# A second graph network whose two layers run interleaved, layer 0 of the next block ahead of layer 1 of this one

## What is computed

```python
def layer(h, params):                      # twice, weights of layer 0 and then of layer 1
    u = jnp.einsum('bid,bjd->bij', h, h) / temper
    a = jax.nn.softmax(u, axis=-1)
    delta = a * adjacency_matrix
    attn = delta / (jnp.sum(delta, axis=-1, keepdims=True) + 1e-10)
    hl, hs, hr = h @ wl.T + b_l, h @ ws.T + b_s, h @ wr.T + b_r
    ctx = (attn * upper) @ hl + diag(attn)[..., None] * hs + (attn * lower) @ hr
    o = (ctx - mean) / jnp.sqrt(var + LN_EPS) * g + beta
    return jax.nn.relu(o)
x = layernorm(x + second_network(x, adj))
```

## Time and profile before

| | |
|---|---|
| median of 3 runs | 1693.14 us (1692.88 to 1693.48) |
| the profiled execution | 1695.46 us, of which its span is 1693.6 us |
| PE busy | 1668.7 us, 99% of the span |
| DVE, ACT, POOL busy | 1267.6 us (75%), 956.0 us (56%), 623.2 us (37%) |
| chain that ended last | PE 93%, DVE 3%, ACT 1%, POOL 1%, DMA 1%, issue 1% |
| granted TensorE clock, mean | 0.995 of full speed |

### The profile page before, as it was taken

The page is one execution under the profiler, slowest core; times in us unless marked ns, Lnnn a source line. Parts: engine busy times, 40 slices in busy tenths (PEclk is TensorE's granted clock), DMA queues, the critical chain, the costliest instruction groups (busy, mean ns, idle before and its releaser), DMA issues.

```text
span 1693.6 us, 29852 instructions
## 1 busy us (share of the span) xinstructions
PE 1668.7 (99%) x9684; PEld 1580.2 (93%) x9684; DVE 1267.6 (75%) x2778; ACT 956.0 (56%) x2009; POOL 623.2 (37%) x668
## 2 busy tenths in 40 slices
PE   9999999999999999999999999999999999999995
PEld 8989989889899899899999999999999999999995
DVE  5587685867859678695887968769687686877866
ACT  5645455364554645546566665565655656656654
POOL 5243252433424233243523514434153351523505
PEclk9999999999999999999999999999999999999998
DMA  5215021020300203003104140400304004040101
GB/s 160 77 30 158 6 71 53 25 93 6 109 14 25 93 6 118 6 25 94 49 15 97 41 96 0 118 0 22 96 22 96 0 25 92 22 96 0 49 30 38
DMA packets 108074, 92.02 MB, mean 54 GB/s; under 512 B 63360, under 2 KB 101248, under 8 KB 108032
## 3 DMA queue, kind: packets, MB, share of 16 engines
q1 hardware_dynamic: 108032, 91.51, 19.1%
HBM read 66.33 MB, written 25.17 MB: 54 GB/s over the span
## 4 chain that ended last, share of the span: by engine, by line
PE 93%; DVE 3%; ACT 1%; POOL 1%; DMA 1%; issue 1%; SPq 0%; ACTq 0%; DVEq 0%
PE b_work L1228 33%; PE b_work L377 23%; PE b_work L402 11%; PE b_score_ps L392 8%; PE b_work L1241 8%; PE b_work L413 4%; PE b_score_ps L119 3%; PE b_turn L360 1%; PE b_turn L1185 1%; PE b_score_ps L1204 1%; DMA b_z<-in_L_gnn_W_lin 1%; PE b_score_ps L1201 0%; POOL g_qv_lo L663 0%; PE b_turn L1212 0%; PE b_score_ps L1185 0%
## 5 line engine op out<-in xcount | busy, mean ns | idle before, releaser
L1228 PE MATMUL b_work<-b_w_hi,b_ht 128*128 128x384 f32 x2304 | 605.2, 337 | 0.5 <-ACT b_work L1327 0.3
L1228 PEld LDWEIGHTS b_work<-b_w_hi,b_ht 128*128 128x128 f32 x2304 | 417.5, 188 | 1.7 <-ACT b_work L1327 1.2
L1228 PE MATMUL b_work<-b_w_lo,b_ht 128*128 128x384 f32 x1152 | 385.3, 334 | 0.0
L377 PE MATMUL b_work<-b_ht,b_w_hi 128*128 128x512 f32 x1134 | 350.5, 390 | 0.7 <-DVE g_qv_lo L782 0.7
L663 POOL TENSOR_TENSOR g_qv_lo<-g_v_full,g_qv_hi 128x384 fp32r<-128x384 f32 x128 | 132.8, 1057 | 359.2 <-ACT g_qv_hi L533 359.2
L377 PEld LDWEIGHTS b_work<-b_ht,b_w_hi 128*128 128x128 f32 x1134 | 211.8, 188 | 41.8 <-issue 1.1
L377 PE MATMUL b_work<-b_ht,b_w_lo 128*128 128x512 f32 x567 | 221.6, 391 | 0.0
L1228 PEld LDWEIGHTS b_work<-b_w_lo,b_ht 128*128 128x128 f32 x1152 | 216.5, 188 | 0.0
L1633 DVE TENSOR_TENSOR s_v_lo<-b_work,s_v_hi 128x384 fp32r<-128x384 f32 x256 | 140.7, 555 | 90.3 <-ACT s_v_hi L1333 86.6
L402 PE MATMUL b_work<-b_w_hi,b_ht 128*128 128x384 f32 x768 | 206.1, 335 | 0.0
L1327 ACT ACTIVATE b_work<-b_bias 128x384 f32<-128x384 f32 x256 | 126.4, 494 | 140.0 <-DVE b_z L1671 104.5
(11 more groups left out here) (174 smaller groups left out, 3288.1 us busy)
## 6 DMA issues: line engine op xcount, KB each, us to landing
g_x_res<-in_x SPq DMA_DIRECT2D x16, 768.0 KB, 7.7
b_x_in<-x SPq DMA_DIRECT2D x64, 192.0 KB, 6.7
s_x_res<-x SPq DMA_DIRECT2D x16, 768.0 KB, 7.3
b_x_in<-in_x_t SPq DMA_DIRECT2D x15, 768.0 KB, 8.9
out<-b_z SPq DMA_DIRECT2D x15, 768.0 KB, 3.8
x<-b_z SPq DMA_DIRECT2D x14, 768.0 KB, 3.9
b_a_tr<-in_adj_t SPq DMA_DIRECT2D x64, 64.0 KB, 3.3
g_a_nat<-in_adj SPq DMA_DIRECT2D x32, 64.0 KB, 2.4
```

What stands on the lines that cost most here:

```text
L377: mm = pe.matmul(bank[:], w, h, start=(n == 0), stop=(n == len(pairs) - 1))
L1228: mm = pe.matmul(bank[:, 0:H], h, w, start=(n == 0 and side == 2), stop=(n == len(pairs) - 1), skip_group_check=True)
```

## The change

- The units are ordered anew. `layer_of`, `block_of`, `stream_of` and `pair_of` now say what a unit is: serial number 0 is layer 0 of block 0; then odd units are layer 0 of block k + 1 and even units are layer 1 of block k; the last unit (number 31) is layer 1 of block 15.
- The rows between the layers of one block go from `z[1]` to a DRAM tensor `z_rows` and from there, in four DMAs, into `x_in[0]` (`pass_rows_on`), and `flip_block` turns them there, for 14 of the 16 layer-1 units. The layer-1 units 2 and 31 are still turned by TensorE (`turned_by_tensor`), from rows that `normalise` writes to `x_in`.
- In the unit ahead of a layer-1 unit the turning stands earlier on ScalarE and VectorE (`early`).
- A buffer `z[unit % 2]` holds a unit's output. `contexts_out` waits for `z_stored` in layer 0 and for the store of the previous output block in layer 1. SyncE's order, `masks` and `final_normalise` follow the new order of units.
- With the block transposes the features of layer 1 come in another order, so the layer-1 weights, gain and shift are loaded in quarters: four DMAs in place of one each.
- TensorE's pass 0 stands ahead of its loop.

```diff
             def next_tables():
+                for out_, row in ((sh.gain_f, next_ln_w[0]), (sh.shift_f, next_ln_b[0])):
+                    parts = row.rearrange("(q k p) -> q p k", q=QUADS, k=KO)
+                    for q in range(QUADS):
+                        sp.dma_start(out_[quarter(q)], parts[q], allow_slow_non_contiguous=True).then_inc(next_small, 16)
...
+    FINAL = PASSES * UNITS - 1
+
+    def serial(i, unit):
+
+        return i * UNITS + unit if isinstance(i, int) else None
+
+    def layer_of(i, unit):
+        if serial(i, unit) in (0, FINAL):
+            return int(serial(i, unit) == FINAL)
+        return 1 - unit % 2
+
+    def block_of(i, unit):
+        if serial(i, unit) in (0, FINAL):
+            return 0 if serial(i, unit) == 0 else PASSES * STREAMS - 1
+        return (i + unit // UNITS) * STREAMS + (-1, 1, 0, 2)[unit % UNITS]
+
+    def stream_of(i, unit):
+        if serial(i, unit) in (0, FINAL):
+            return int(serial(i, unit) == FINAL)
+        return (1, 1, 0, 0)[unit % UNITS]
+
+    def pair_of(i, unit):
+
+        if serial(i, unit) in (0, FINAL):
+            return (0, 0) if serial(i, unit) == 0 else (PASSES - 1, 1)
+        back, s = ((-1, 1), (0, 1), (0, 0), (1, 0))[unit % UNITS]
+        step = unit // UNITS + back
+        return (i + step if step > 0 else i - 1 if step < 0 else i), s
+
+    def turned_by_tensor(i, unit):
+
+        return serial(i, unit) in (2, FINAL)
...
+            def load_x(i, unit):
+
+                sp.wait_ge(turned, nth(i, unit - 2, KO, KO - 1))
+                for q in range(QUADS):
+                    sp.dma_start(sh.x_blocks[unit % 2][quarter(q)], x_b[(*pair_of(i, unit), q)])\
+                        .then_inc(x_loaded[unit % 2], 16)
+
+            def pass_rows_on(i, unit):
+
+                k = block_of(i, unit)
+                sp.wait_ge(z_ready, (k + 1) * NT)
+                sp.dma_start(z_v, z[unit % 2][:, :, 0:H]).then_inc(z_stored, 16)
+                sp.wait_ge(z_stored, k * 16)
+                for q in range(QUADS):
+                    sp.dma_start(sh.x_blocks[1 - unit % 2][quarter(q)], z_b[q]).then_inc(x_loaded[1 - unit % 2], 16)
 
             def load_adj(i, s):
+
+                sp.wait_ge(keep_ready[s], i + 1)
                 for b in range(2):
                     h = slice(b * 64, b * 64 + 64)
-                    sp.dma_start(a_tr[s][h, :, h], adj_t_v[i, s, b]).then_inc(adj_loaded[s], 16)
+                    sp.dma_start(a_tr[s][h, :, h], adj_t_v[i + 1, s, b]).then_inc(adj_loaded[s], 16)
+
...
+            def first_pass():
+                load_residual(0, 0)
+                load_adj(0, 0)
+                load_residual(0, 1)
+                pass_rows_on(0, 1)
+                load_x(0, 5)
+                load_adj(0, 1)
+                store_last(0)
+                store_last(1)
+
+            def one_pass(i):
+                store_out(i - 1, 2)
+                pass_rows_on(i - 1, 3)
+                load_x(i, 3)
+                load_adj(i, 0)
+                load_residual(i, 0)
+                store_out(i, 0)
+                pass_rows_on(i, 1)
+                load_x(i, 5)
+                load_adj(i, 1)
+                load_residual(i, 1)
+
...
             def turn_block(i, unit, k):
+                pe.wait_ge(z_ready, (block_of(i, unit) + 1) * NT)
                 if k < 2:
                     pe.wait_ge(prob_lo_ready, nth(i, unit - 1, 2, k))
                 else:
                     pe.wait_ge(sums_ready, nth(i, unit - 1, 1, 0))
+                rows = x_in[block_of(i, unit) % 2]
                 for t in range(NT):
-                    mm = pe.transpose(turn_banks[k][:, t * P:(t + 1) * P], z[s][:, t, k * P:(k + 1) * P], eye)
+                    mm = pe.transpose(turn_banks[k][:, t * P:(t + 1) * P], rows[:, t, k * P:(k + 1) * P], eye)
                 mm.then_inc(turned, 1)
...
             def turn_out(i, unit, k):
-                bank = turn_banks[k]
+                bank = turn_banks[k] if turned_by_tensor(i, unit) else flipped[k % 2]
...
             def normalise(i, unit, tiles):
+                    rows, out_ = z[s][:, t, 0:H], z[s][:, t, 0:H]
+                    if serial(i, unit) in (0, FINAL - 2):
+
+                        rows = rows.rearrange("p (q k f) -> p k q f", q=QUADS, k=KO)
+                        out_ = x_in[block_of(i, unit) % 2][:, t, :].rearrange("p (k q f) -> p k q f", q=QUADS, k=KO)
+                    nc.scalar.activation(out_, rows, ACT.Identity, scale=rstd[:, t:t + 1],
...
             def second_half(i, unit, more, tail):
-                flip_next = more and layer_of(unit + 1) == 0
-                turn_next = more and layer_of(unit + 1) == 1
+                turn_next = more and turned_by_tensor(i, unit + 1)
+                early = more and not turn_next and layer_of(i, unit + 1) == 1
+                late = more and layer_of(i, unit + 1) == 0
                 probabilities_hi(i, unit)
+                if early:
+                    turn_out(i, unit + 1, 0)
                 value_hi(i, unit, 6)
                 seed(i, unit, 9)
-                if flip_next:
+                if early:
+                    turn_out(i, unit + 1, 1)
+                if late:
                     turn_out(i, unit + 1, 0)
                 value_hi(i, unit, 7)
                 seed(i, unit, 10)
-                if flip_next:
+                if early:
+                    turn_out(i, unit + 1, 2)
+                if late:
                     turn_out(i, unit + 1, 1)
                 if turn_next:
                     turn_out(i, unit + 1, 0)
                     turn_out(i, unit + 1, 1)
                 value_hi(i, unit, 9)
-                if more:
+                if late or turn_next:
                     turn_out(i, unit + 1, 2)
                 value_hi(i, unit, 10)
...
             def masks(i, s, first=False):
-                    pool.wait_ge(own_ready, nth(i, 2 + s - UNITS, 1, 0))
+                    pool.wait_ge(own_ready, nth(i, 2 * s - 2, 1, 0))
...
             def one_pass(i, last, first=False):
-                    if unit == 0 and not first:
-                        final_normalise(1)
-                    if unit == UNITS - 1 and not last:
-                        final_normalise(0)
+                    if layer == 0 and not (first and unit < 3):
+                        final_normalise(unit - 1, stream_of(i, unit - 1))
...
-                    if not last and unit % STREAMS == 1:
-                        masks(i + 1, unit // STREAMS)
+                    if layer == 0 and unit > 0 and not last:
+                        masks(i + 1, unit // 2)
...
             def flip_block(i, unit, k):
+                dve.wait_ge(x_loaded[s], 16 * QUADS * (block_of(i, unit) + layer_of(i, unit)))
...
+            def contexts_out(i, unit, tiles=range(NT)):
+
+                s, k = unit % 2, block_of(i, unit)
+                if layer_of(i, unit) == 0:
+                    wait(dve, z_stored, (k - 1) * 16)
+                elif serial(i, unit) not in (2, FINAL):
+                    other = 1 - stream_of(i, unit)
+                    dve.wait_ge(stored[other], before[other] + 16 * (i + unit // UNITS))
...
             def up_to_contexts(i, unit, last, residual, tail=None):
-                flip_next = more and layer_of(unit + 1) == 0
-                turn_next = more and layer_of(unit + 1) == 1
+                turn_next = more and turned_by_tensor(i, unit + 1)
+                flip_next = more and not turn_next
+                early = flip_next and layer_of(i, unit + 1) == 1
...
                 probabilities_lo(i, unit)
+                if early:
+                    turn_lo(i, unit + 1, 0)
+                    flip_block(i, unit + 1, 2)
...
+    z_rows = nc.dram_tensor("z_rows", (TOK, H), F32).ap()
```

More of the change, by code:

```diff
@@ L1134, in _ @@
             load_weight(1)
+            load_x(0, 3)
             sp.wait_ge(split, 1)
@@ L1659, in own_probability @@
                 nc.vector.tensor_reduce(own[:], expo[:], AX.X, ALU.add).then_inc(own_ready, 1)
-            def contexts_out(i, unit, tiles=range(NT), first=False):
-                layer, s = divmod(unit % UNITS, STREAMS)
-                if layer == 0 and not first:
-                    dve.wait_ge(stored[s], before[s] + 16 * (i + unit // UNITS))
+            def contexts_out(i, unit, tiles=range(NT)):
+                s, k = unit % 2, block_of(i, unit)
+                if layer_of(i, unit) == 0:
+                    wait(dve, z_stored, (k - 1) * 16)
+                elif serial(i, unit) not in (2, FINAL):
+                    other = 1 - stream_of(i, unit)
+                    dve.wait_ge(stored[other], before[other] + 16 * (i + unit // UNITS))
                 dve.wait_ge(own_ready, nth(i, unit, 1, 0))
@@ L1777, in final_normalise, with up_to_contexts @@
                                             ALU.mult, ALU.add).then_inc(last_ready, 1)
-            def up_to_contexts(i, unit, last, s, tail=None):
```

(16 more changed lines are left out.)

225 lines of the change are left out of this document (110 added, 115 removed).

## The result

The changed kernel takes 1698.41 us (median of 9 runs, 1696.38 to 1701.54) beside 1692.88 us for the kernel before in the same runs: ratio 1.0034, 95% interval 1.0024 to 1.0044. It is slower by 0.34%, where 1684.9 us and faster had been forecast. The profiled execution took 1701.54 us, the slowest of the nine, with a span of 1699.7.

What follows compares the result with a forecast made beforehand. TensorE, busy throughout every steady unit, was taken as the bound. Turns -18.3, unit 3's stall -0.6, short unit-1 waits -0.8 and new even-unit stalls +11.5 gave -8.2 us: 1693.1 to 1684.9 us, range 1676 to 1691.

Steps and rivals of the forecast that it cites:

- What is removed: TensorE's turning of layer-1 units: 1.31 us a unit, gone from 14 units, 18.3 us less on the path.
- What was priced at nothing: VectorE's added block transposes (2.16 us in 14 units), DRAM round trip, masks: no path time; small DMAs at worst 1 us once.
- What becomes late: contexts_out after a residual delays job 4 in even units: 0.82 us in each of 14, 11.5 us in all.
- C: Start of contexts_out after a unit with a residual, taken as F - 0.62.
- the length of the chain: From contexts_out through variances, maxima, exponentials and seed 4 to TensorE's job 4: 8.50 us, so job 4 at C + 8.50.
- F: Start of the first fold of a unit; job 4 was due at F + 7.38 in a layer-1 unit.
- the extra 0.32 us: Added to job 4's 0.50 us lateness in each such even unit, for two restarts and late seed 7.
- bounds of 7 to 15 us: Total stall of the 14 even units, from 0.5 to 1.1 us each; gives 1680.4 to 1688.4 us.
- Rival D: Even-unit stall larger through what follows it (seed 7, ht for next scores): 1.35 us, not 0.82; 1692.3 us; chance 0.10.
- The sum: Less 18.3, 0.6 and 0.8, plus 11.5: -8.2 us, to 1684.9; odd units 25.09, even 26.39; profiled span 1685.4.
- The range: Whole kernel, 1676 to 1691 us: the stall's bounds stretched to half of the no-stall rival and half of Rival D.
- The chance of slower, 0.10: 0.08 for block transposes costing path time in odd units, 0.02 for rows arriving late from DRAM.

Runs made afterwards that it cites:

- e4: Changed kernel's unit order alone: TensorE turns every layer-1 unit, no DRAM round trip or layer-1 block transposes; 1720.26 us, ratio 1.0161 to the kernel before.
- e3: Changed kernel with VectorE's loop over the middle passes written out, same instructions and order; 1692.22 us, ratio 0.9995 to the kernel before.
- e7: e3 with each block transpose of a layer-1 unit done twice, a wait between the two; 1708.23 us, 16.0 over e3.
- e1: Changed kernel with GpSimd's diagonal waiting until VectorE's offset is through, nothing else changed; 1694.18 us, ratio 1.0003 to the kernel before.
- e2_contexts_first: Changed kernel with VectorE's final statistics, variance and offset behind contexts_out, variances and row maximum, GpSimd reordered to match; 1685.03 us, ratio 0.9956 to before.

## Why the prediction was wrong, point by point

- **What is removed** was right: 1.31 us an odd unit (e4 against e3: 1.34), odd units of 25.10 us. Unit 3, which is layer 0 now, has no stall (26.21 to 25.10).
- **What was priced at nothing** was right for the round trip, whose stores and loads landed in 3.5 and 3.7 us with no wait of VectorE for a DMA, and for the masks. It was right for the block transposes as they are, but by e7 some 1.0 us more is all that fits.
- **What becomes late**: C and the length of the chain were right to 0.01 us. `contexts_out` starts at 1046.66, which is F - 0.45 on this timeline and F - 0.61 in the chain's frame (forecast F - 0.62), and job 4 comes 1055.17 - 1046.66 = 8.51 later (forecast 8.50).
- **The step that failed is the extra 0.32 us** for "the two restarts and the following, equally late seed 7". It came from unit 3 of pass 0. That unit has no final normalise on GpSimd ahead of the diagonal, and VectorE's offset there meets nothing (0.15 us at 927.77 in the kernel before). In the new even units the normalise of 2.61 us pushes the diagonal onto the offset, and seed 7 comes 0.81 us later still. So the extra is 1.04 us and not 0.32, and an even unit lost 1.54 to 1.56 us and not 0.82; over the forecast that is 6.3 us in the nine ordinary ones and 0.7 in unit 30. Without the third wait the term was sound: 26.43 us in the loop of e1, where the sum has 26.39. By the bounds of 7 to 15 us it was outside, at 14 x 1.54 = 21.6. Rival D had the place (seed 7) and nearly the price (1.35), and its 1692.3 us is what e3_vector_unrolled took, 1692.2. That is luck in part: D has no word of what holds seed 7 up.
- **The other failure is a term that wasn't there**: the gaps at VectorE's jump back. Units 10, 14, 18 and 22 took 115.4 us in place of 4 x 26.39 = 105.6: 9.9 us in the profiled execution. The kernel before shows only 0.36 us at that place, and the added instructions were counted for their busy time, not for what they do to the length of a loop.
- **The sum again**: 6.3 + 0.7 + 9.9 = 16.9 us over the forecast; the span was 1699.7 against 1685.4, 14.3 over. Of the 2.6 us left, 1.9 are the tail behind the last unit's fold, 42.8 us against 44.7 before; the rest wasn't traced.
- **The range** had no room for both terms: with only one of them left the time is still 1692 (e3) or 1694 (e1), just outside of it. The chance of slower, 0.10, was put on odd units and transfers, neither of which moved.

What stays open: why the clock falls behind some of the 2 us stalls and not others. That the lock on a port pair is what stretches the offset is the skill's explanation; the runs show that the stretch ends with the diagonal and goes when the two are kept apart. One record doesn't fit as it stands: in unit 2 the offset takes 0.15 us (at 923.85) while the record of a GpSimd root on 128x4 elements runs from 923.12 to 924.13.

## What to carry to other kernels

Where a chain decides how late a unit starts, ask what the other engines will be doing at the moment each small instruction of it runs: a 0.15 us instruction took 1.2 us because GpSimd's final normalise had pushed an instruction of 1.3 us onto it, and the unit taken as a model has no such normalise. Count the instructions of a loop's body, waits included, before adding to it. And put work that nobody waits for (final statistics) behind the step that starts the critical chain: here that order and an unrolled loop turned a loss of 0.3% into a gain of 1.2%.

## What the runs showed of the hardware

- A VectorE instruction of 128x4 elements with two SBUF inputs: 0.15 us alone, 1.21 to 1.28 us in the changed kernel when it starts 0.05 to 0.11 us behind a GpSimd instruction on 128x512 that reads SBUF, and its end falls on that one's end. It took 0.36 to 0.47 us in the kernel before during GpSimd's normalise of 128x384 tiles.
- VectorE's loop: 0.36 and 0.35 us at the jump back with bodies of 486 and 507 instructions, 2.8 to 3.1 us with 519 and 520, and 18 instruction fetches of 8 KB in 350 us in place of none.
- A TensorE stall of 2.0 to 2.1 us was followed in two of four cases of one execution by a granted clock of 0.64 and 0.52 over 2.8 us (units 10 and 18), which made the stall's cost 2.5 us in place of 1.0. By the length of the unit it was so in three of four in e1_diag_later (stalls of 1.9 to 2.2 us) and in two of four in e2_contexts_first (2.3 to 2.5 us).
- Of 2.16 us added to VectorE in an odd unit, where it is busy for 20 of 25 us, 0.77 came onto the path at once and 0.38 in the unit behind it (e7): the average room of 5 us says little.
